# Splitting the experts' third weight into fp16 pairs once, during attention, and keeping the pairs in DRAM

## The reference

```python
h = rmsnorm(x, ff_ln_w)
ht = h.reshape(-1, Dx)                       # 1024 tokens x 256
logits = ht @ gate_w
top_vals, top_idx = jax.lax.top_k(logits, K) # K = 2 of E = 8
gates = jax.nn.softmax(top_vals, axis=-1)
for e in range(E):
    we = jnp.sum(gates * (top_idx == e), axis=-1)
    ye = jax.nn.silu(ht @ w1[e]) * (ht @ w3[e]) @ w2[e]   # 256 -> 896 -> 256
    out = out + we[:, None] * ye
```

## Time and profile before

| | us |
|---|---|
| median of 3 runs | 681.04 (678.54 to 684.99) |
| the profiled execution, its own time | 683.2 |
| its span on the core | 681.4 |
| PE busy | 507.7 (75% of the span) |
| DVE busy | 512.9 (75%) |
| ACT busy | 356.4 (52%) |
| POOL busy | 264.3 (39%) |

### The profile page before, as it was taken

The page is one execution under the profiler, slowest core; times in us unless marked ns, Lnnn a source line. Parts: engine busy times, 40 slices in busy tenths (PEclk is TensorE's granted clock), DMA queues, the critical chain, the costliest instruction groups (busy, mean ns, idle before and its releaser), DMA issues.

```text
span 681.4 us, 9298 instructions
## 1 busy us (share of the span) xinstructions
PE 507.7 (75%) x3018; PEld 345.2 (51%) x3018; DVE 512.9 (75%) x970; ACT 356.4 (52%) x758; POOL 264.3 (39%) x219
## 2 busy tenths in 40 slices
PE   2011296789999999997189989999999998046763
PEld 1001132468888788875145646566656665023442
DVE  4999875788888889872729779879798786379672
ACT  3236145677777778762034554635734554256452
POOL 3465024744444456415180683633350500530001
PEclk9999998799999999997579989999999999667685
DMA  8200003040000000004811942351443110210000
GB/s 269 99 0 0 0 1 123 5 158 1 2 1 1 1 1 25 9 1 141 257 39 28 313 85 44 120 148 29 173 144 117 25 23 16 79 53 8 16 16 24
DMA packets 28362, 44.23 MB, mean 65 GB/s; under 512 B 4795, under 2 KB 21435, under 8 KB 28059
## 3 DMA queue, kind: packets, MB, share of 16 engines
q1 hardware_dynamic: 20843, 31.43, 14.2%
q0 software_dynamic: 3072, 8.14, 5.0%
q10 hardware_dynamic: 4400, 4.06, 1.7%
HBM read 38.51 MB, written 5.12 MB: 64 GB/s over the span
## 4 chain that ended last, share of the span: by engine, by line
PE 52%; DVE 24%; ACT 8%; issue 7%; POOL 5%; DMA 1%; SPq 0%; ACTq 0%; DVEq 0%; POOLq 0%
PE pb L407 10%; PE pw L407 8%; PE pb L583 7%; PE sc L446 6%; PE sc L583 5%; PE po L407 4%; PE pt L457 3%; PE sc L659 2%; PE pb L659 2%; DVE areg L1077 2%; DVE areg L1063 2%; DVE areg L1061 2%; PE pt L592 1%; POOL breg L1626 1%; DVE areg L1410 1%
## 5 line engine op out<-in xcount | busy, mean ns | idle before, releaser
L583 PE MATMUL pb<-wreg,areg 128*128 x184 | 85.1, 606 | 0.8 <-ACT areg L898 0.8
L407 PE MATMUL pb<-areg,wreg 128*128 128x512 f16 x240 | 63.5, 404 | 14.3 <-ACT breg L800 9.0
L1598 POOL TENSOR_TENSOR breg<-breg,con 128x512 f32<-128x512 f32 x32 | 40.6, 1270 | 83.5 <-ACT breg L800 83.5
L407 PE MATMUL pw<-areg 128*128 128x256 f16 x406 | 59.5, 283 | 7.7 <-DVE areg L1418 7.7
L583 PE MATMUL sc<-wreg,areg 128*128 x184 | 63.2, 486 | 0.0
L808 ACT ACTIVATE breg<-breg,mx 128x128 f32<-128x128 f32 (+1 forms) x128 | 56.6, 445 | 1.6 <-DVE mx L1185 1.6
L583 PEld LDWEIGHTS pb<-wreg,areg 128*128 128x128 f32 x184 | 33.9, 195 | 36.3 <-issue 36.1
L407 PEld LDWEIGHTS pw<-areg 128*128 128x128 f16 x406 | 40.7, 101 | 18.3 <-DVE areg L1418 11.2
L446 PE MATMUL sc<-areg,breg 128*128 128x128 f32 (+1 forms) x256 | 47.7, 330 | 0.4 <-DVE mx L1185 0.4
L1640 POOL DMA_INDIRECT areg<-h_dram,row_ids x23 | 31.5, 1371 | 40.6 <-PE po L575 22.4
L1593 POOL TENSOR_TENSOR breg<-breg 128x512 f32<-128x512 f32 x32 | 44.4, 1388 | 4.5
(11 more groups left out here) (239 smaller groups left out, 1285.8 us busy)
## 6 DMA issues: line engine op xcount, KB each, us to landing
wreg<-in_L_ffn_w SPq DMA_DIRECT2D x24, 896.0 KB, 7.9
ys_dram<-areg ACTq DMA_DIRECT2D x23, 128.0 KB, 1.8
wreg<-in_L_ffn_wq SPq DMA_DIRECT2D x1, 2048.0 KB, 9.3
wreg<-in_L_ffn_wo SPq DMA_DIRECT2D x1, 2048.0 KB, 8.2
areg<-in_fside_BxSxS ACTq DMA_DIRECT2D x4, 256.0 KB, 5.7
x_in<-in_x SPq DMA_DIRECT2D x4, 256.0 KB, 5.4
h_dram<-areg SPq DMA_DIRECT2D x8, 128.0 KB, 1.7
out_dram<-areg SPq DMA_DIRECT2D x8, 128.0 KB, 1.7
```

What stands on the lines that cost most here:

```text
L407: last = nc.tensor.matmul(bank, w(a), m(b), start=first and k == 0, stop=final and k == 2)
L583: last = nc.tensor.matmul(bank, xsT[:, parity, c * P:(c + 1) * P], wreg[:, bass.ds(base + (m * C + c) * FF + lo, w)], start=c == 0, stop=c ...
L1598: G.tensor_tensor(t2[:, parity, :].rearrange("p (b n) -> p b n", b=2), t2[:, parity, :].rearrange("p (b n) -> p b n", b=2), rope_sin.rearr ...
```

## The change

The split of w2 leaves the expert tiles. SP now loads the fp32 `w2` of one expert at a time into SBUF (`w2_words`) while attention runs. ACT makes the high part in steps 4, 8, ..., 32 (after `o_high`), DVE the low part one step later (after `o_low`), and SP writes both to a new DRAM tensor `w2_dram`. `load_expert` fetches the third piece from there: the same 896 KB, now as one contiguous run a partition. PE's `down` reads the pair from the ring `wreg`, at an address held in a register, where it read from fixed buffers before. The load of expert 0 is issued after all eight pairs have been written.

```diff
+W2_STEPS = tuple(range(4, 4 + 4 * NE, 4))
...
-            eng.dma_start(wreg[:, base + 2 * n:base + WEXP].rearrange("p (c n) -> p c n", c=FC),
-                          t["L0_ffn_w2"][e].rearrange("(c p) n -> p c n", p=P)).then_inc(s_w[e % RING], 16)
+            eng.dma_start(cut(wreg, base + 2 * n, FC * D, F16).rearrange("p (s n) -> p s n", s=2), w2_dram[e])\
+                .then_inc(s_w[e % RING], 16)
...
+            for e in range(NE + 1):
+                if e >= 1:
+                    sp.wait_ge(s["w2lo_done"], e)
+                    for k in range(2):
+                        sp.dma_start(w2_dram[e - 1][:, k], w2_half[k]).then_inc(s["w2_out"], 16)
+                elif e == 0:
+                    sp.wait_ge(s["rat_done"], B)
+                if e < NE:
+                    sp.dma_start(w2_words.rearrange("p (c n) -> p c n", c=FC), t["L0_ffn_w2"][e].rearrange("(c p) n -> p c n", p=P))\
+                        .then_inc(s["w2_in"], 16)
             sp.wait_ge(s["wolo_done"], 4)
+            sp.wait_ge(s["w2_out"], 32 * NE)
             load_expert(sp, 0)
...
-                pe.wait_ge(s["w2lo_done"], n + 1)
...
-                    last = split_products(pw[:, 0:D], lambda a: hhT[:, a, c, :], lambda a: w2s[parity][a][:, c, :], c == 0, c == FC - 1)
+                    last = split_products(pw[:, 0:D], lambda a: hhT[:, a, c, :],
+                                          lambda a: wreg[:, bass.ds(base + 2 * C * FF + (a * FC + c) * D // 2, D // 2)].bitcast(F16),
+                                          c == 0, c == FC - 1)
...
+            def w2_high(e):
+                act.wait_ge(s["w2_in"], 16 * (e + 1))
+                if e >= 1:
+                    act.wait_ge(s["w2_out"], 32 * e)
+                nc.scalar.activation(w2_half[0], w2_words, ACT.Copy, scale=WS).then_inc(s["w2hi_done"], 1)
...
+                if u in W2_STEPS:
+                    w2_high(W2_STEPS.index(u))
...
-                    w2_high(n, parity)
...
+                if u - 1 in W2_STEPS:
+                    w2_low(W2_STEPS.index(u - 1))
...
-                w2_low(n, n % 2)
```

More of the change, by code:

```diff
@@ L135, in build @@
         hhT = cut(areg, 2816, FF, F16).rearrange("p (s c n) -> p s c n", s=2, c=FC)
-        w2s = [[cut(region, at, FC * D // 2, F16).rearrange("p (c n) -> p c n", c=FC) for region, at in parts]
-               for parts in (((areg, 4224), (areg, 5120)), ((areg, 6016), (breg, 5120)))]
+        w2_words = cut(areg, 11264, FC * D)
+        w2_half = [cut(areg, at, FC * D // 2, F16) for at in (13056, 16896)]
         ysb = cut(areg, 3712, 2 * D).rearrange("p (k n) -> p k n", k=2)
@@ L225, in build @@
         row_ids = sb("row_ids", [P, MT], I32)
+        w2_dram = nc.dram_tensor("w2_dram", (NE, P, 2, FC * D), F16).ap()
         h2_dram = nc.dram_tensor("h2_dram", (NT * P, D), F32).ap()
@@ L248, in build @@
             "w_ready xT_done xT_copied upa_done upb_done silu_a_done silu_b_done inner_a_done inner_b_done "
-            "hT_done hT_copied hTlo_done w2hi_done w2lo_done down_done y_copied "
+            "hT_done hT_copied hTlo_done w2_in w2_out w2hi_done w2lo_done down_done y_copied "
             "x1_ready sgx_ready qx_ready qxT_done qxT_copied gatep_done upp_done gate_ready inner_ready "
@@ L593, in h_transposes, with down @@
                 last.then_inc(s["hT_done"], 1)
-            def down(n, parity, piece=None):
+            def down(n, base, piece=None):
                 pe.wait_ge(s["hTlo_done"], n + 1)
-                pe.wait_ge(s["w2lo_done"], n + 1)
                 if not isinstance(n, int) or n >= 1:
@@ L618, in _ @@
                 parity = n % 2
+                if n >= 1:
+                    last_base = base
                 if n < MT:
@@ L632, in _ @@
                 if n >= 1:
-                    down(n - 1, 1 - parity, y_slot.get(n))
+                    down(n - 1, last_base, y_slot.get(n))
             def quantised_transposes(i):
@@ L902, in _ @@
             copy_xT(0, 0)
-            def w2_high(n, parity):
-                e = act.value_load(tmi[0:1, bass.ds(n, 1)], min_val=0, max_val=NE - 1)
-                act.wait_ge(s["w_ready"], e + 1)
-                if not isinstance(n, int) or n >= 2:
-                    act.wait_ge(s["down_done"], n)
-                nc.scalar.activation(w2s[parity][0].rearrange("p c n -> p (c n)"),
-                                     wreg[:, bass.ds((e % RING) * WEXP + 2 * C * FF, FC * D)], ACT.Copy, scale=WS).then_inc(s["w2hi_done"], 1)
             for k in range(2):
@@ L1208, in wo_low, with w2_low @@
                 V.scalar_tensor_tensor(wo16[:, 1, hs], stage_wo[:, hs], WS, wo16[:, 0, hs], ALU.mult, ALU.subtract).then_inc(s["wolo_done"], 1)
+            def w2_low(e):
+                dve.wait_ge(s["w2hi_done"], e + 1)
+                V.scalar_tensor_tensor(w2_half[1], w2_words, WS, w2_half[0], ALU.mult, ALU.subtract).then_inc(s["w2lo_done"], 1)
             def second_norm(i):
@@ L1404, in silu @@
                 V.tensor_tensor(hh[:, lo:hi], silu_out[:, lo:hi], b, ALU.mult).then_inc(done, 1)
-            def w2_low(n, parity):
-                e = dve.value_load(tmi[0:1, bass.ds(n, 1)], min_val=0, max_val=NE - 1)
-                dve.wait_ge(s["w2hi_done"], n + 1)
-                V.scalar_tensor_tensor(w2s[parity][1].rearrange("p c n -> p (c n)"),
-                                       wreg[:, bass.ds((e % RING) * WEXP + 2 * C * FF, FC * D)], WS,
-                                       w2s[parity][0].rearrange("p c n -> p (c n)"), ALU.mult, ALU.subtract).then_inc(s["w2lo_done"], 1)
             def hT_low(n):
```

## The result

| | before | after |
|---|---|---|
| median of the runs | 684.19 us (678.54 to 687.63, 6 runs) | 693.63 us (692.39 to 701.51, 6 runs) |
| ratio, 95% interval | | 1.0159, 1.0123 to 1.0195 |
| profiled execution, its span | 683.2, 681.4 | 693.26, 691.3 |

The changed kernel is 1.6% slower by the ratio, some 11 us; the two medians lie 9.4 us apart. (With three more runs the median of the kernel before is 684.2 and no longer the 681.0 that the prediction started from.) I had forecast +4.3 us (0.6%); 693.6 lies inside the range of 675.5 to 695.0, near its upper end. The sign was right and the size was not.

What follows compares the result with a forecast made beforehand. The prediction took PE to set the pace in attention and, except for a few waits for DVE, in the expert tiles. From 681.0 us, +13.1 (attention) - 8.8 (tiles) + 0 (PE) gave 685.3 us, range 675.5 to 695.0.

Steps and rivals of the forecast that it cites:

- PE's own cost: In the expert tiles: 14 register instructions of 46 ns per tile stay hidden behind the sequencer's lead; cost 0.
- rival 3: In the expert tiles: the register instructions are not hidden, 14.8 us more, 700 us in all; chance 0.06.
- What the tiles give back, 8.8: In the expert tiles: PE's waits for DVE shrink, 1.7 + 4.6 + 2.5 = 8.8 us gained.
- The terms of 1.7 and 2.5: In the expert tiles: PE's wait before 361.68 goes (1.7 us), and those at 444.08 and 503.47 go (2.5 us).
- the chain to 403: Expert tiles: PE's 3.33 us wait before 403.04, through four engines, shrinks to 0.54 and slow matmuls recover; gain 4.6 us.
- rival 4: In the expert tiles: nothing is given back since other waits replace DVE's; 692 us in all; chance 0.10.
- Attention, 13.1: In attention: the split costs 1.2 for expert 0, 6 x 1.6, and 2.3 for expert 7, together 13.1 us.
- the bound: In attention: the nearest lower bound, from step 22's projections 0.59 us over a unit, 8 x 0.6 = 4.8 us.
- The hold-up of DVE by POOL: In attention: DVE's low part stands still until POOL's instruction ends, running from 213.7 to 215.75, ending 2.0 us behind POOL.
- expert 0's 1.2: In attention at step 4: expert 0's split costs 0.1 us for ACT and 1.1 for DVE, 1.2 together.
- rival 1: Attention swallows the split: 4.8 us or less lost, 677.0 us in all, 672.2 if nothing is lost; chance 0.22.
- rival 2: In attention: DVE's low part and POOL collide more, row maxima late, 2.6 us an expert, 693 us; chance 0.14.

Runs made afterwards that it cites:

- experiment 4: Kernel before, with the down projection's 14 addresses taken from a register read anew in each tile; 685.85 us, ratio 1.0033.
- experiment 5: Changed kernel without register addresses: every tile reads expert 0's third weights from one fixed place; 687.89 us, ratio 1.0085 to the kernel before.
- experiment 6: Changed kernel with PE's read of the next tile's expert moved ahead of the second up projection; 691.55 us, ratio 1.0112 to the kernel before.
- experiment 11: Changed kernel with early expert read and the split in 28 pieces, ACT's behind the exponentials, DVE's behind `normalise`; 673.89 us, ratio 0.9853 to the kernel before.
- experiment 13: As experiment 11, but DVE's piece at the end of its step, in front of the next rotary product; 679.36 us, ratio 0.9938 to the kernel before.
- experiment 14: Experiment 11 run once more, on another chip; 672.23 us, ratio 0.9852 to the kernel before.
- experiment 1: Kernel before with only tile 0 splitting w2 and all tiles using that pair, no register instructions added; 676.15 us, ratio 0.9927.
- experiment 10: Changed kernel with splits at steps 4, 7, 10, 13, 16, 24, 28 and 32, none just before the residual; 689.11 us, ratio 1.0101 to the kernel before.
- experiment 9: Changed kernel with whole instructions moved, ACT's behind the exponentials, DVE's behind `normalise`; 687.88 us, ratio 1.0100 to the kernel before.
- experiment 2: Kernel before with the split and its transfers added in attention, while the tiles still split for themselves; 694.48 us, ratio 1.0184.
- experiment 3: Kernel before with the down projection's addresses formed from one register holding 0 for all tiles; 682.53 us, ratio 1.0014.
- experiment 7: Kernel before with only PE's read of the next tile's expert moved ahead of the second up projection; 685.95 us, ratio 1.0015.

## Why the prediction was right in sign and wrong in size

- **PE's own cost, "Cost 0": this step failed, and it made the miss.** The term is 5.8 us (experiments 4 to 6). I had put the read of the expert 0.6 us later, the bare sum of 14 x 46 ns. It moved by 1.3: the instructions last 55 ns, and they stand among 42 weight loads and matmuls which the sequencer issues in turn with them (the 14 spread over 1.9 us, 571.3 to 573.2). And I had ended the walk at the read's own 0.55, while 0.9 pass from the start of the read to `pb`'s first register instruction. 532.4 + 1.3 + 0.9 = 534.6 lies behind the 534.48 at which the array was through, and further behind the moment at which `pb`'s weights were loaded before the change. The sign that I had set for rival 3, 21 matmuls of over 2.4 us, could not have shown it: these took 2.50 us at 503.31 and 2.47 there before, and the time is lost behind them. Rival 3 had the right mechanism with a price of 14.8, every nanosecond of the 14 instructions paid; only what goes beyond the lead is paid, 5.8 us or about two fifths of it.
- **What the tiles give back, 8.8.** Without the late read the tiles gave back 6.4 us in experiment 6, 6.8 in experiment 5 (with the last 21 matmuls put at the 3.79 of before), and 5.9, 4.6 and 8.7 in experiments 11, 13 and 14; the scatter between executions is as large as the miss. The terms of 1.7 and 2.5 came, 2.0 (the second tile took 9.29 us instead of 11.24 in experiments 5 and 6) and 2.9 (experiment 1). The failed one is the chain to 403, 1.9 instead of 4.6: with DVE freed a wait of 1.8 to 2.5 us stayed in most profiled executions and one of 0.5 in two (experiments 10 and 14); what decides between them was not settled. The note that this chain goes through four engines stood under rival 4, and should have halved the term.
- **Attention, 13.1.** The sum held, 12.0 for experts 1 to 7 against 11.9; the parts did not. A usual expert cost 1.12, not 1.6: ACT's part 0.23 instead of 0.5, DVE's 0.89 instead of 1.05. Expert 4 cost 3.66 since it stood one step before the residual, which I had looked at the earlier trace rows for a bound and not as a neighbour (experiment 10), expert 5 1.9 for a reason that was not looked for, and expert 7 about 2.0 (2.3 forecast). Errors that cancel are no confirmation of the walk; that the sum held was luck. The bound itself was misread: the chain's row at 239.27 is not where the projection began. In the timeline it begins at 239.11, 5.99 us behind the one before and 0.43 over a unit, so the bound was 3.4 us and not 4.8.
- **The hold-up of DVE by POOL** was as walked: 2.76 us in place of 2.03, ending 1.9 us behind POOL's end (2.0 forecast), and 2.01 where POOL is idle (experiment 9). The Trainium skill (SBUF — State Buffer, section "Who interferes with whom") gives an exclusive lock for a DVE instruction with two SBUF inputs beside a GpSimd instruction that reads; the traces agree here, in both orders: in experiment 13 DVE's piece waits where POOL came first (up to 1.75 us for 0.68), and POOL's instruction where DVE did (1.58 for 1.27); at expert 0 of the changed kernel DVE came first too, and POOL's took 2.90.
- **Expert 0, the loads and `h2`.** In the profile of the changed kernel expert 0's 1.2 can't be told from the differing distances of the first units. In those of experiments 2, 5 and 10 these distances are the ones of before, and the seventh is 6.44 to 6.46 us instead of 6.00: expert 0 cost 0.45. The load of expert 0 and the writes of `h2` cost little, as held: the stretch to the first expert matmul was 0.8 longer in the changed kernel's profile, but it took 34.9 and 35.4 in experiments 1 and 3, which have the code of before there, and 34.2 in experiment 10, which has the changed one.
- Rivals 1 and 2 were both partly true: attention can swallow all of the split (experiment 11: nothing lost), and pays 3.7 where DVE's row maxima come late. Which of them one gets is decided by the size of the instruction and by its place.

With the terms as measured (12.0 + 0.45 for attention, 6.4 for the tiles and 5.8 for the sequencer) the sum would have been 12.5 - 6.4 + 5.8 = +11.9, against 9.4 by the medians and some 11 by the ratio.

## What to carry to other kernels

Count an engine's sequencer as a resource of its own: when a change adds register instructions, find the next point at which the sequencer has to finish a read before the array can go on, and compare its lead there with the whole way from the read to the first matmul behind it. Reading the next tile's index one phase earlier cost nothing (experiment 7) and gave back 5.8 us of the tiles. Work that is to vanish in another engine's waits must be cut to the size of the wait and put into it: the same conversion cost 12 us as eight whole instructions at the end of a step, 6 us as eight in the right place, and nothing as 28 pieces.

## What was not expected of the hardware

- Addresses that come out of a register cost nothing at the matmul; 14 instructions that compute them, 55 ns each, pushed the read behind them back by 1.3 us (1.9 us after the first weight load instead of 0.6).
- The end of the kernel differs by execution and not by version: the same program took 96.1 us for it in one execution and 99.1 in another (experiments 11 and 14). Its repeating unit lasts 5.92 us in some places and some 7.6 in others. In the profile before, the unit of 5.91 that starts at 645.8 lies in 10 us with a granted clock of 0.99, the one of 7.60 behind it in 10 us with 0.83; but in experiment 10 a unit of 7.51 lies in 10 us with 1.00, so the clock goes with it mostly and not always. Near attention's start the sixth and seventh projections come after 5.7 and 5.5 us in some executions (before) and after 7.2 each in others (experiment 11). Each of the two makes 3 to 5 us between executions, which is why stretches and not only totals were compared.
- The same 21 matmuls behind the same wait of 2.6 us ran in 2.46 us with a granted clock of 1.00 over the 6 us that hold them (experiments 1 and 5), or in 3.63 to 4.12 with 0.72 (the changed kernel, experiment 11).
